# Two sets of transposes per chunk of keys, placed in steps 2 and 5 of a group instead of 2 and 3

## The reference, cut to what matters

```python
xn = _gn(x)                                   # mean and variance over 8 channels x 4096 pixels
f = Wq @ xn + bq; g = Wk @ xn + bk            # 32 x 4096
h = Wv @ xn + bv                              # 256 x 4096
s = einsum('bki,bkj->bij', f, g)              # 4096 x 4096
beta = softmax(s, axis=1)
x = x + gamma * einsum('bci,bij->bcj', h, beta)
```

## Time and profile before

| | |
|---|---|
| median of 3 runs | 2545.13 us (2543.74 to 2546.59) |
| span of the profiled execution, first to last instruction | 2539.4 us |
| TensorE busy | 2371.8 us, 93% of the span |
| VectorE busy | 1956.3 us, 77% |
| ScalarE busy | 1751.0 us, 69% |
| GpSimd busy | 492.5 us, 19% |
| mean granted clock of TensorE | 0.978 of full speed |
| DMA | 36.66 MB, 14 GB/s on average |

### The profile page before, as it was taken

The page is one execution under the profiler, slowest core; times in us unless marked ns, Lnnn a source line. Parts: engine busy times, 40 slices in busy tenths (PEclk is TensorE's granted clock), DMA queues, the critical chain, the costliest instruction groups (busy, mean ns, idle before and its releaser), DMA issues.

```text
span 2539.4 us, 52331 instructions
## 1 busy us (share of the span) xinstructions
PE 2371.8 (93%) x17098; PEld 1662.9 (65%) x17098; DVE 1956.3 (77%) x3421; ACT 1751.0 (69%) x2841; POOL 492.5 (19%) x810
## 2 busy tenths in 40 slices
PE   4999999988899999998899999999889999999977
PEld 3677777772467777775256777777525777777742
DVE  8877777758877777775887777786688677877677
ACT  4677777767657777776666777677665777777765
POOL 2211111105511111100541111110153111111025
PEclk9999999999999999998999999999899999999989
DMA  2000000000000000000100000000010000000001
GB/s 89 2 9 8 8 8 8 9 18 34 35 1 9 8 8 8 8 18 9 42 27 1 9 8 8 11 14 10 14 45 19 1 0 0 0 0 0 2 12 55
DMA packets 18836, 36.66 MB, mean 14 GB/s; under 512 B 1296, under 2 KB 2192, under 8 KB 18704
## 3 DMA queue, kind: packets, MB, share of 16 engines
q1 hardware_dynamic: 18704, 34.99, 4.0%
HBM read 18.21 MB, written 16.78 MB: 14 GB/s over the span
## 4 chain that ended last, share of the span: by engine, by line
issue 72%; PE 9%; POOL 8%; DVE 8%; ACT 2%; POOLq 1%; DMA 0%; DVEq 0%; SPq 0%; ACTq 0%
POOL r L709 2%; PE acc L992 2%; DVE ph L521 2%; PE sps L963 2%; POOL r L712 2%; PE acc L963 2%; DVE htl L515 2%; DVE htl L529 1%; POOL mrow L710 1%; POOL r L711 1%; PE tps L998 1%; POOLq L194 1%; PE sps L1170 1%; PE sps L1166 1%; POOL xl L694 1%
## 5 line engine op out<-in xcount | busy, mean ns | idle before, releaser
L836 ACT ACTIVATE ph<-sps,esc 128x512 f16<-128x512 f32 x1024 | 704.0, 688 | 388.5 <-PE sps L1004 378.4
L1048 PE MATMUL acc<-hth,ph 128*128 128x257 f16 x4096 | 959.8, 274 | 1.0 <-ACT ot L827 0.9
L1049 PE MATMUL acc<-htl,ph 128*128 128x256 f16 x4096 | 958.4, 273 | 0.0
L450 DVE TENSOR_REDUCE mx<-tps 128x512 f32 (+1 forms) x1024 | 701.0, 688 | 290.8 <-PE tps L998 287.1
L491 DVE TENSOR_TENSOR pl<-p,ph 128x512 f16<-128x512 f32 x1024 | 699.5, 684 | 104.5 <-ACT p L837 104.5
L837 ACT ACTIVATE p<-sps,esc 128x512 f32<-128x512 f32 x1024 | 697.6, 681 | 0.0
L1058 PE MATMUL acc<-hth,pl 128*128 128x257 f16 x4096 | 621.5, 274 | 1.9
L1058 PEld LDWEIGHTS acc<-hth,pl 128*128 128x128 f16 x4096 | 397.7, 98 | 154.3 <-DVE pl L491 9.6
L1049 PEld LDWEIGHTS acc<-htl,ph 128*128 128x128 f16 x4096 | 401.8, 98 | 134.6 <-issue 1.3
L1048 PEld LDWEIGHTS acc<-hth,ph 128*128 128x128 f16 x4096 | 401.8, 98 | 80.2 <-ACT ot L827 21.4
L998 PE MATMUL tps<-fst,gst 96*128 96x512 f16 x1024 | 388.3, 384 | 11.0 <-DVE mx L450 6.1
(11 more groups left out here) (209 smaller groups left out, 1949.6 us busy)
## 6 DMA issues: line engine op xcount, KB each, us to landing
xa<-x SPq DMA_DIRECT2D x32, 512.0 KB, 3.6
out<-og SPq DMA_DIRECT2D x32, 512.0 KB, 2.7
og<-w SPq DMA_DIRECT2D x1, 608.0 KB, 4.4
p<-wv SPq DMA_DIRECT2D x1, 256.0 KB, 3.2
w1n<-w SPq DMA_DIRECT2D x1, 128.0 KB, 2.9
wqn<-wq SPq DMA_DIRECT2D x1, 96.0 KB, 2.1
wkn<-wk SPq DMA_DIRECT2D x1, 96.0 KB, 2.1
selh<-sel SPq DMA_DIRECT2D x1, 76.0 KB, 4.6
```

Source lines behind the costliest of these rows:

```text
L450: V.reduce_max(mx[:, ds(tile, 1), c], tps[par][:], AX).then_inc(t_free, 1)
L836: A(ph[:, u % SLOTS], sps[u % 2][:], ACT.Exp, scale=esc[:]).then_inc(ph_ok, 1)
L1048: mm(acc[j][:, 0:C + 1], w, hth[:, t], start=(t == 0), stop=False)
L1049: mm(acc[j][:, 0:C], w, htl[:, t], start=False, stop=False)
```

## The change

Steps 2 and 3 of a finishing group become steps 2 and 5, on TensorE and VectorE alike. The first half is transposed, added and counted as before (steps 2, 2 and 3). The second half is transposed and added in step 5 and its statistics stand in step 6. The place of `next_stats` (steps 6 and 7) stays as it is, and nothing in SyncE's program is edited.

```diff
+BACK_AT = (2, 5)
...
-                    if finish and u in (2, 3):
-                        if u == 2:
+                    if finish and u in BACK_AT:
+                        if u == BACK_AT[0]:
                             dve.wait_ge(bv_ok, b + 1)
-                        finish_block(b * NCH + J - 1, J - 1, u - 2)
-                    if finish and u in (3, 4):
-                        stats(b * NCH + J - 1, J - 1, u - 3)
+                        finish_block(b * NCH + J - 1, J - 1, BACK_AT.index(u))
+                    if finish and u - 1 in BACK_AT:
+                        stats(b * NCH + J - 1, J - 1, BACK_AT.index(u - 1))
                     if finish and u in (6, 7):
                         next_stats(b, J - 1, u - 6)
...
-                    if finish and u in (2, 3):
+                    if finish and u in BACK_AT:
                         n = b * NCH + J - 1
                         if maxima:
                             pe.wait_ge(t_free, N + u + 1)
-                        transposed(n, u - 2)
+                        transposed(n, BACK_AT.index(u))
...
-                    if finish and u in (2, 3):
-                        pe.wait_ge(x1_ok, 2 * n + u - 1)
+                    if finish and u in BACK_AT:
+                        pe.wait_ge(x1_ok, 2 * n + BACK_AT.index(u) + 1)
```

## The result

The changed kernel takes 2590.32 us (median of 4 runs, 2588.68 to 2591.71) against 2544.43 for the kernel before. The ratio is 1.018, with a 95% interval of 1.0165 to 1.0194, so it is slower by 46 us. The forecast was 2576.9 with a range of 2566 to 2588: the direction and the main mechanism came out as said, and the time lies 2.3 us above the range. The span of the profiled execution is 2588.4 in place of 2539.4, 49.0 more.

What follows compares the result with a forecast made beforehand. TensorE, busy 93% of the span, bounds ordinary steps; in finishing groups it waits for VectorE. 28.6 + 5.8 - 6 x 0.43 = +31.8 us on the span of 2539.4, with 5.7 carried over: 2576.9 us, range 2566 to 2588.

Steps and rivals of the forecast that it cites:

- The gain of step 4: In finishing groups with maxima, TensorE's step 4 no longer waits for VectorE's maximum: 0.43 us gained per group.
- The standing of VectorE: VectorE idles before next_stats in step 6, awaiting the load: 18 times about 2.1 us, 3 times about 2.6, some 46.
- the chain's two parts: From the second half's addition to SyncE's issue of the load 0.91 us, from issue to VectorE's use 3.55.
- the walk: Step-by-step timing of one finishing group with the second half in step 5: 1.59 us more in chunks 1 to 6.
- What reached TensorE: Step 7's piece and last products wait for VectorE: 1.59 us more per finishing group of chunks 1 to 6, 28.6 in all.
- Chunk 7: Finishing group without maxima: VectorE's wait for the load makes it 1.92 us longer, three times, 5.8 us.
- The clock: TensorE's granted clock around step 7's wait: the forecast sum holds no term for a fall.
- Rival 3: TensorE's clock falls in step 7's wait, at most about half of 9 us in 21 groups, 95 us, 2671; 3%.
- The base: Whole kernel: the profiled span of 2539.4 us lies 5.7 below the median of 2545.1, carried over to the forecast.

Runs made afterwards that it cites:

- Experiments 1: Changed kernel (transposes in steps 2 and 5) with next_stats moved to steps 2 and 5 of the following group: 2531.53 us, ratio 0.9949.
- 2: Kernel before (transposes in steps 2 and 3) with next_stats moved to steps 2 and 5 of the following group: 2541.95 us, ratio 0.9996.
- 3: Changed kernel with the statistics of steps 6 and 7 reading xs, already there, without the load's semaphore; loads still made: 2538.89 us, ratio 0.9985.
- 4: Changed kernel with the next chunk's load split into two 256 KB halves, each with its own semaphore: 2536.81 us, ratio 0.9975.
- experiments 5: Kernel before, transposes kept in steps 2 and 3, with next_stats moved from steps 6 and 7 to 4 and 5: 2577.04 us, ratio 1.0135.
- 7: Changed kernel with both next_stats in step 7 in place of steps 6 and 7: 2550.92 us, ratio 1.0039.
- Experiments 6: Changed kernel with 12 more zero-matrix matmuls on TensorE in step 7 of finishing groups with maxima: 2582.88 us, ratio 1.0161.
- 9: Changed kernel with 5 more zero-matrix matmuls on TensorE in step 7 of finishing groups with maxima: 2577.31 us, ratio 1.0137.

## Why the prediction was right in its main part and too low

**The gain of step 4** was right: L1034 no longer waits. In the last image the six groups are 2.3 us shorter together (2.6 forecast; step 7 takes 1.80 to 1.84 in five of them), and the whole stage 2.7. Experiments 1 and 2 show that the gain belongs to the transposes' place.

**The standing of VectorE** was right: 44.0 us in 21 stands against 46, with the chain's two parts within 0.14 of the forecast. Experiments 1, 3 and 4 take it away in three ways and each gets the attention stages back to about 470; experiments 5 and 7 give two other doses, with the cost that the walk gives (2577 forecast without falls, 2577.0 measured; 2552 forecast, 2550.9 measured).

**What reached TensorE** was mis-sized a little: 1.69 us per group without a fall in place of 1.59, 18 x 0.10 = 1.8 us, since step 7 scatters from 3.67 to 4.19 with the landings. Chunk 7 gave 5.9 in place of 5.8.

**The clock** is the step that failed: the sum put it at nothing. Rival 3 was given 3%, on a single row in which TensorE had idled 1.78 us and kept its clock. That row was of the right length (TensorE idled 1.40 to 1.93 us in the long steps), but one row can't tell "never" from "sometimes", and the prediction let the clock fall in all groups or in none. In fact it fell behind 7 of 18 stands, and cost 3.40 - 1.69 = 1.7 us each there, 12.0 us. Without these the median would have been 2578.3, inside the range. The price I had put on it, half of 9 us, was too high as well: it came from a stretch in which TensorE had little to do. Experiments 6 and 9 show that idling in the stand causes it: more work in the same stand, and 0 of 18 fall, twice, where 7 and 6 of 18 fell without it; experiment 5's shorter stands had none in 21. Why the clock falls behind one such stand and not behind the next stays open. The Trainium skill, TensorE: Matmul & The Clock Gate, section HAM oscillation, tells of a kernel whose waits for a DMA throw the clock back in each pass of a loop. Those waits were longer than the stands here, so the prediction was wrong to say that this rival would hold by that rule; here the clock fell in 7 and 6 of 21 passes.

**The base.** The account on the spans is 31.8 forecast, 12.0 for the falls, 1.8 and 0.1 for the steps, 1.7 at the start of the second image's attention and 1.5 in the stages outside of it, where the clock's low stretches fell otherwise than before: 48.9 of 49.0. These last 3.2 were seen and not tested. The profiled execution of before seems itself to have been short: I carried over 5.7 us from its span to the median, while the changed kernel's median lies 1.9 above its profiled span (2590.32 and 2588.4). By luck this difference of 3.8 works against the rest: the forecast is 17.2 us too low on the span (49.0 against 31.8), but only 13.4 on the median (2590.3 against 2576.9).

## What to carry to other kernels

When work is moved later on one engine, look for what it releases on a queue that the change doesn't touch, and for who waits for that: here one addition moved by two steps put a load's 4.5 us into VectorE's queue, in front of unrelated instructions that TensorE needed. The cure was to move the use as well, by a group, which made both moves together 0.5% faster than the kernel before. A stall of TensorE of 1.5 to 1.8 us cost about twice its length when the clock fell behind it (3.40 against 1.69 us), so price such a stall as sometimes one and sometimes the other, and not by one row.

## What the runs showed of the hardware that was not expected

The clock's fall depended on more than the length of a stand: steps 7 of 3.81, 4.01 and 4.10 us were followed by a slow step, others of 3.95, 4.01 and 4.13 were not, and between two executions of the same kernel all but one of the groups changed. Work without any use (the products with a matrix of zeros of experiments 6 and 9) held the clock where idling let it fall.

Half a chunk (256 KB) landed in 2.7 us against 3.6 for 512 KB. An estimate from these two sizes, if the time grows evenly with the size, is that 1.8 us of a load don't depend on it (3.6 - 2 x 0.9). It is no rule for other transfers: the stores of 512 KB landed sooner than the loads of that size in the changed kernel.

```profile
xa<-x SPq DMA_DIRECT2D x32, 512.0 KB, 3.6
out<-og SPq DMA_DIRECT2D x32, 512.0 KB, 2.8
```
